# Shared experts: router logits with the router weights as the stationary operand, 512 tokens moving

## The reference

```python
x = _layernorm(x).reshape(-1, 512)                       # 4096 tokens
shared_out = silu(x @ shared_gate_w) * (x @ shared_up_w) @ shared_down_w   # inner width 1024
logits = x @ gate_w                                      # 32 experts
topk_ids = jnp.argmax(logits, axis=-1)
topk_val = jnp.max(logits, axis=-1)
scores = jax.nn.sigmoid(topk_val)[:, None]
xs = x * scores                                          # goes to the routed experts, sorted by topk_ids
```

## Time and profile before

| | |
|---|---|
| median of 3 runs | 3218.11 us (3213.92 to 3230.29) |
| the profiled run, whole time | 3221.88 us |
| its span, first to last instruction | 3220.2 us |
| stage `shared_experts` in it | from about 1660 to 2314 us |
| TensorE busy over the span | 2922.3 us, 91% |
| VectorE, ScalarE, GpSimd busy | 63%, 48%, 32% |
| mean granted clock of TensorE | 0.965 of full speed |

### The profile page before, as it was taken

How to read it: one execution, slowest core, us unless ns; L and a number is a source line. 1 busy time by engine, 2 the same in 40 slices (tenths; PEclk the granted TensorE clock), 3 DMA queues, 4 the chain that set the end, 5 groups by cost and what they waited for, 6 DMA issues and landing times. The chain is left out here.

```text
span 3220.2 us, 46395 instructions
## 1 busy us (share of the span) xinstructions
PE 2922.3 (91%) x13572; PEld 2351.9 (73%) x13573; DVE 2039.7 (63%) x2656; ACT 1558.1 (48%) x2683; POOL 1025.1 (32%) x637
## 2 busy tenths in 40 slices
PE   6888988998958999999959999999769999999998
PEld 5666766776846777777747888888558888888886
DVE  7888788778556556555543333333488674767776
ACT  5656665665745555555531111111236563655555
POOL 4767766776831111111100000000023232323323
PEclk9999999999989999999979999999879999999999
DMA  1000000000040111111031111111368684768765
GB/s 56 23 7 23 23 23 10 23 23 10 11 140 27 40 39 51 41 40 39 27 102 59 56 52 52 52 52 52 118 242 298 222 309 169 267 220 295 275 241 197
DMA packets 185543, 322.71 MB, mean 100 GB/s; under 512 B 23656, under 2 KB 42088, under 8 KB 185472
## 3 DMA queue, kind: packets, MB, share of 16 engines
q1 hardware_dynamic: 173680, 295.56, 26.8%
q0 software_dynamic: 11792, 26.25, 2.4%
HBM read 286.86 MB, written 46.66 MB: 104 GB/s over the span
## 5 line engine op out<-in xcount | busy, mean ns | idle before, releaser
L153 POOL TENSOR_TENSOR a_pL<-a_p,a_pH 128x1024 fp32r<-128x1024 f32 x256 | 627.7, 2462 | 271.5 <-DVE a_p L319 268.5
L1403 DVE TENSOR_TENSOR e_wL<-e_raw,e_wH 128x1024 fp32r<-128x1024 f32 x384 | 450.2, 1217 | 34.1 <-PE d_pU L1618 24.0
L1398 ACT CAST e_wH<-e_raw 128x1024 fp32r<-128x1024 f32 x384 | 385.0, 1053 | 122.8 <-PE d_pD L49 64.1
L319 DVE TENSOR_TENSOR a_p<-a_r,a_pS 128x1024 f32<-128x1024 f32 x256 | 310.8, 1219 | 166.3 <-ACT a_r L160 162.4
L160 ACT ACTIVATE a_r<-a_pS 128x1024 f32<-128x1024 f32 x256 | 262.5, 1025 | 260.9 <-PE a_pS L49 260.9
L715 POOL TENSOR_TENSOR b_S<-b_S,b_ri 128x1024 f32<-128x1024 f32 x64 | 121.5, 1899 | 558.8 <-DVE b_ri L812 558.8
L47 PE MATMUL a_pS<-a_qH,a_kH 128*128 (+1 forms) x512 | 215.7, 421 | 87.7 <-DVE a_p L319 86.8
L160 ACT ACTIVATE a_pH<-a_r 128x1024 fp32r<-128x1024 f32 x256 | 271.5, 1061 | 9.1
L1271 POOL MEMSET r_ones<- 128x128 bf16 x1 | 0.2, 206 | 657.7 <-POOLq L980 657.7
L47 PE MATMUL a_pO<-a_pH,a_vH 128*128 128x512 f32 x512 | 203.3, 397 | 0.6 <-POOL a_pL L153 0.6
L48 PE MATMUL a_pO<-a_pL,a_vH 128*128 128x512 f32 x512 | 203.4, 397 | 0.0
(11 more groups left out here) (291 smaller groups left out, 7640.7 us busy)
## 6 DMA issues: line engine op xcount, KB each, us to landing
e_raw<-in_L_ffn_routed_gate_w SPq DMA_DIRECT2D x256, 256.0 KB, 4.2
e_raw<-in_L_ffn_routed_up_w SPq DMA_DIRECT2D x256, 256.0 KB, 5.3
e_raw<-in_L_ffn_routed_down_w SPq DMA_DIRECT2D x128, 512.0 KB, 6.3
a_xb<-in_x SPq DMA_DIRECT2D x8, 1024.0 KB, 5.6
x<-a_o SPq DMA_DIRECT2D x32, 256.0 KB, 2.3
b_xb<-x SPq DMA_DIRECT2D x32, 256.0 KB, 2.7
b_xr<-x SPq DMA_DIRECT2D x32, 256.0 KB, 3.1
x<-b_xr SPq DMA_DIRECT2D x32, 256.0 KB, 2.7
```

Of the source, the lines that this page charges most:

```text
L153: nc.gpsimd.tensor_tensor(pL[:, j % RING, :, :], p[:, j % 2, :, :], pH[:, j % RING, :, :].bitcast(F32), ALU.subtract).then_inc(s["low"], 1)
L319: v.tensor_tensor(p[:, j % 2, :, :], r[:, j % 2, :, :], pS[j % 2][:, :, :], ALU.mult).then_inc(s["p"], 1)
L1398: copy(self.wH[:, n, :, :], self.raw[:, n, :, :]).then_inc(self.s["high"], 1)
L1403: unit.tensor_tensor(self.wL[:, n, :, :], self.raw[:, n, :, :], self.wH[:, n, :, :].bitcast(self.F32), self.sub).then_inc(self.s["low"], 1)
```

## The change

The logits of a group are computed with the router weights stationary and the 512 tokens moving. High and low part of the router weights stand side by side in one tile `rHL`, 64 columns, so one matmul gives high by high in output rows 0 to 31 and low by high in rows 32 to 63; four further matmuls of 32 columns add high by low to rows 0 to 31. The result (64 by 512) goes into `pX`'s bank under the name `pL`, ScalarE copies it to SBUF (`lt`), and four transposes behind the up product of chunk 1 bring it into `pR` with tokens on the partitions. VectorE adds the two halves into `lg` and routes from that. The routing moves from chunk 0 to chunk 1, the score from chunk 1 to 2, the scaling from chunk 2 to 3. TensorE's wait on `own` moves from before the logits to before the up product of chunk 1, beside a new wait there for `lt`.

```diff
-        rw, (rH, rL) = sb("rw", [P, KC, EXP]), (sb(n, [P, KC, EXP], F32R) for n in ("rH", "rL"))
+        rw, rHL = sb("rw", [P, KC, EXP]), sb("rHL", [P, KC, 2, EXP], F32R)
+        rH, rL = rHL[:, :, 0, :], rHL[:, :, 1, :]
+        lt, lg = sb("lt", [2 * EXP, GTOK]), sb("lg", [P, GT, EXP])
...
-        pX, pR = ps("pX", [P, KC, P]), ps("pR", [P, GT, EXP])
+        pX, pR = ps("pX", [P, KC, P]), ps("pR", [P, GT, 2, EXP])
+        pL = pX[0:2 * EXP, :, :].rearrange("p a c -> p (a c)")
...
-        RL = 4
+        RL = 5
...
-                    if i == 1:
+                    if i == 2:
                         act.wait_ge(s["top"], g + 1)
                         nc.scalar.activation(score[:, :], top[:, :], ACT.Sigmoid).then_inc(s["score"], 1)
...
                     nc.scalar.activation(hH[:, i, :], h[:, i % 2, :], ACT.Copy).then_inc(s["hH"], 1)
+                    if i == 0:
+                        act.wait_ge(s["logit_ps"], g + 1)
+                        wait(act, s["logit"], g)
+                        nc.scalar.activation(lt[:, :], pL, ACT.Copy).then_inc(s["lt"], 1)
...
-                nc.vector.tensor_reduce(top[:, :], pR[:, :, :], axis=AX.X, op=ALU.max).then_inc(s["top"], 1)
+                link(nc.vector.tensor_reduce(lg[:, :, :], pR[:, :, :, :].rearrange("p t i e -> p t e i"), axis=AX.X, op=ALU.add))
+                nc.vector.tensor_reduce(top[:, :], lg[:, :, :], axis=AX.X, op=ALU.max).then_inc(s["top"], 1)
                 dve.wait_ge(s["top"], g + 1)
-                link(nc.vector.tensor_tensor(rank[:, :, :], pR[:, :, :], wide(top[:, :]), ALU.is_equal))
+                link(nc.vector.tensor_tensor(rank[:, :, :], lg[:, :, :], wide(top[:, :]), ALU.is_equal))
...
-                    if i == 0:
+                    if i == 1:
                         route(g)
-                    if i == 2:
+                    if i == 3:
                         scale(g)
...
             def logits(g):
-                pe.wait_ge(s["own"], SL + RL * g)
+                wait(pe, s["lt"], g)
+                both = lambda a: nc.tensor.matmul(pL, rHL[:, a, :, :].rearrange("p i e -> p (i e)"), xH[:, a, :], start=a == 0, stop=a == KC - 1)
+                for a in range(KC - 1):
+                    both(a)
+                for a in range(KC):
+                    nc.tensor.matmul(pL[0:EXP, :], rH[:, a, :], xL[:, a, :], start=False, stop=False)
+                m = both(KC - 1)
+                m.then_inc(s["logit_ps"], 1)
+
+            def logit_transposes(g):
                 for t in range(GT):
-                    for a in range(KC):
-                        at = (slice(None), a, slice(t * P, (t + 1) * P))
-                        m = split_matmuls(nc, pR[:, t, :], (xH[at], xL[at]), (rH[:, a, :], rL[:, a, :]), a == 0, a == KC - 1)
+                    m = nc.tensor.transpose(pR[:, t, :, :].rearrange("p i e -> p (i e)"), lt[:, t * P:(t + 1) * P], ident[0:2 * EXP, 0:2 * EXP])
                 m.then_inc(s["logit"], 1)
...
+                    if i == 1:
+                        pe.wait_ge(s["lt"], g + 1)
+                        pe.wait_ge(s["own"], SL + RL * g)
                     hidden(pU[i % 2][:, :], wuH, wuL, i, s["up"])
                     if i == 0:
                         logits(g)
+                    if i == 1:
+                        logit_transposes(g)
```

More of the change, by code:

```diff
@@ L997, in shared_experts @@
         pD = [ps(f"pD{i}", [P, C]) for i in range(2)]
-        pX, pR = ps("pX", [P, KC, P]), ps("pR", [P, GT, EXP])
+        pX, pR = ps("pX", [P, KC, P]), ps("pR", [P, GT, 2, EXP])
+        pL = pX[0:2 * EXP, :, :].rearrange("p a c -> p (a c)")
         s = {n: ctx.enter_context(nc.semaphore("c_" + n)) for n in
-             ("ramp g_in rH rL x_in0 x_in1 r_in0 r_in1 normed xt xH xL gate up sig gated h hH hL logit top own score xs xs_out"
+             ("ramp g_in rH rL x_in0 x_in1 r_in0 r_in1 normed xt xH xL gate up sig gated h hH hL logit_ps lt logit top own score xs xs_out"
               " down sum out0 out1").split()}
         SL = 16
-        RL = 4
+        RL = 5
         parts = []
@@ L1065, in _ @@
             act.wait_ge(s["g_in"], 16)
-            nc.scalar.activation(rH[:, :, :], rw[:, :, :], ACT.Copy).then_inc(s["rH"], 1)
+            nc.scalar.activation(rH, rw[:, :, :], ACT.Copy).then_inc(s["rH"], 1)
             high_parts(act, 0, KC)
@@ L1130, in _ @@
             dve.wait_ge(s["rH"], 1)
-            nc.vector.tensor_tensor(rL[:, :, :], rw[:, :, :], rH[:, :, :].bitcast(F32), ALU.subtract).then_inc(s["rL"], 1)
+            nc.vector.tensor_tensor(rL, rw[:, :, :], rH.bitcast(F32), ALU.subtract).then_inc(s["rL"], 1)
             link = Link(dve, s["own"])
```

## The result

The changed kernel takes 3168.63 us, median of four runs (3168.03 to 3170.33), against 3217.2 us for the kernel before, measured beside it again; the ratio is 0.985 with a 95% interval of 0.9834 to 0.9866. The forecast was 3171.8 us, within 3161 to 3200. The profiled run has a span of 3167.1 us, 53.1 us less than the one of before.

A forecast was written before the change was run, and what follows sets the result against it. TensorE was taken to bound the stage. Replacing 69.6 us of logits and clock loss by 23.3 us gains 46.3 us: 3175.6 us from the profiled run, 3171.8 us against the median, range 3161 to 3200.

The forecast's parts named there:

- The place: In `shared_experts`, TensorE never waits from the second group on, so each us it saves comes off the end.
- The old price: Old logits on TensorE: 69.6 us over eight groups, per group 5.27 us of matmuls and on average 3.43 us of clock.
- The new price: New logits on TensorE, with matmuls, transposes and shape changes: 23.3 us over the eight groups.
- The eight matmuls: New logit matmuls with 512 tokens moving: 0.233 us each, 1.87 us a group.
- the transposes: Four added transposes bringing the logits into `pR`: 0.44 us a group.
- the changes of shape: Six switches of stationary columns or rows a group on TensorE: 0.10 us each, 4.8 us in all.
- the drain rival: Every switch of matmul shape empties TensorE's array: 16.8 us instead of 4.8, giving 3183.8 us; chance 0.14.
- The clock: TensorE's clock stays up around the new logits, so its loss of 3.43 us a group goes.
- The rival at 3199.2 us: TensorE's clock falls all the same, costing 3.43 us a group, 27.4 us in all; chance 0.11.
- The cover of the wait: TensorE's new wait for `lt` before chunk 1's up product: margin 1.8 us, cost nothing.
- Several passes: Narrow logit blocks take four passes, 0.93 us a matmul: no gain to speak of, about 3216 us; chance 0.04.
- unpipelined blocks: Narrow blocks in four passes, each new instruction also waiting 0.35 us for array and load: 3245 us, slower; chance 0.02.

## Why the prediction was right

**The place.** TensorE was the bound of the stage and stays it: its three waits are those of before, and each us saved there came off the end.

**The old price.** 69.6 us was right for the profile it was read from. What the prediction didn't say is that 27.4 of it, the clock's share, is one draw: the run with the routing moved drew 24.2 for the same instructions. The gain was forecast at 46.3 us and came out at 48.6 by the first medians, and at 46.0 by those taken with the repeat (3216.32 - 3170.28); by the terms now known it would be 66.4 - 19.0 = 47.4 us from the one profile and 50.6 from the other. That the forecast came so near is in part luck: the price it took off was that of a profiled run 3.8 us above its median, and the new price was 4.3 us too high, so the two errors point against each other.

**The new price.** 23.3 us were forecast, 19.0 measured. The eight matmuls: 1.87 against 1.84 us a group, right; the transposes 0.44, right for the full shape (0.90 - 2 x 0.233 = 0.43). The mis-sized term is the changes of shape: forecast at 0.10 us each, six a group, 4.8 us in all. The four between column widths cost nothing visible, the two to 64 rows and back 0.15 us together where they stand, so about 1.2 us in all, and over a whole group, beside the kernel with full shapes, nothing (71.19 against 71.22 us). The upper bound of 16.8 us, and with it the drain rival at 3183.8, was far off. The Trainium skill's TensorEngine Tiling (Array Packing), section Tiling Modes, says that a change of mode drains TensorE; the 0.10 us step ahead of the transposes could be such a drain, and between 128, 64 and 32 stationary columns this trace shows none. Whether those are changes of mode in the page's sense, no row says.

**The clock.** That it stays up was the weakest step, and it held. The runs show more than the prediction gave as its reason: thin work of 1.7 us in one stretch, and of 5.3 us in four, leaves it up too, and 5.5 us of narrow but dense work as well. In this kernel it took both, thin moving sides and a long stretch, to bring it down while TensorE was never idle. One thing the runs don't separate: the thin matmuls move few columns, and they also keep the weight loads busy all the time (5.27 of 5.27 us, against 4.51 of 5.60 in ordinary work), and the new layout changed both at once. The fall in the first group, behind a wait with loads in 0.83 of 3.40 us, speaks for the few columns; no run tests it. The rival at 3199.2 us had no mechanism left after that.

**The cover of the wait.** The margin was forecast at 1.8 us and is 2.0; the run with the copy late shows what it is worth. The moved routing, scaling and store brought no new wait of TensorE, as the run with these alone shows.

**Several passes, unpipelined blocks.** Not seen: a narrow matmul's pitch is 0.230 us, where they needed 0.93 and more, so the rivals at 3216 and 3245 us are out. That a thin matmul's pitch of 0.110 us is set by its weight load was argued from the rows; no run tests it.

About half of the gain, 23 us, is thus shorter work and the other half, 24 to 27 us, the clock. Had the logits stayed as they were and only been spread, half of it would have been had without any new instruction.

## What to carry to other kernels

Where a stretch of TensorE work has few moving columns behind full weight loads, read the granted clock of the whole stretch and of what stands behind it: here 5.3 us of thin matmuls cost up to 4.9 us more in clock. In the third group of the kernel before the ordinary matmuls behind them paid all of it; in the eighth the thin ones themselves lasted 7.82 us (2239.30 to 2247.12) and so paid about half. Put the small matrix on the stationary side and the long one on the moving side; where that can't be, cut the thin work into short pieces between dense ones. And when the price is read from one profile, take the clock's part of it as one draw out of several.

## What was not expected of the hardware

- How much the same 48 thin matmuls cost in clock varies from group to group between 1.6 and 4.9 us (windows of 12.49 to 15.73 us), and the pattern over the groups differs between two profiles of the same TensorE work.
- A stop of 1.24 us in every group doesn't bring the clock down (1.00 in the windows). Behind the first group's wait for weights it stayed up in the two profiles in which the wait was 1.7 us (the changed kernel's first, and the one with the copy late) and fell to 0.50 in those in which it was 1.9 to 2.1 us (among them the kernel before and the repeat of the changed one). With the logits in pieces it fell behind a wait of 0.9 us, with a thin piece just ahead of it.
- Changing between 128, 64 and 32 stationary columns has no visible price, and narrow blocks even stand a little closer (0.230 against 0.233 us).
